# Sixteen heads in a loop over eight pairs, or written out in each engine's program

## What is computed

```python
xn = _layernorm(x, axis=-1)
x = x + attn(xn, Wq, Wkv, Wo, bo) + ffn(xn, gate_W_packed, gate_scales, up_W_packed, up_scales,
                                        down_W_packed, down_scales)
# attn: 16 heads of 32, 4 key/value heads, causal, ALiBi bias, softmax
scores = jnp.einsum('brgtd,bgsd->brgts', qg, k) / jnp.sqrt(jnp.float32(HD))
attn = jax.nn.softmax(jnp.where(causal, scores + bias, -jnp.inf), axis=-1)
out = jnp.einsum('brgts,bgsd->brgtd', attn, v)
# ffn: weights of 4096 x 512 stored as 4-bit codes with a scale for each block of 32
inter = gelu(xt @ Wg.T) * (xt @ Wu.T)
out = inter @ Wd.T
```

## Time and profile before

| | |
|---|---|
| median of three timed runs | 1851.26 us (1844.19 to 1851.6) |
| span of the profiled execution, first to last instruction | 1858.9 us |
| what lies around that span | not given for the profiled execution |
| PE busy | 1758.1 us, 95% of the span |
| DVE busy | 1468.6 us, 79% |
| ACT and POOL busy | 998.6 us and 980.1 us |
| mean granted TensorE clock | 0.980 of full speed |

### The profile page before, as it was taken

How to read it: one execution, slowest core, us unless ns; L and a number is a source line. 1 busy time by engine, 2 the same in 40 slices (tenths; PEclk the granted TensorE clock), 3 DMA queues, 4 the chain that set the end, 5 groups by cost and what they waited for, 6 DMA issues and landing times. The chain is left out here.

```text
span 1858.9 us, 32744 instructions
## 1 busy us (share of the span) xinstructions
PE 1758.1 (95%) x8528; PEld 964.3 (52%) x8528; DVE 1468.6 (79%) x2619; ACT 998.6 (54%) x1722; POOL 980.1 (53%) x785
## 2 busy tenths in 40 slices
PE   4989999999999999999999999999999999999948
PEld 3755555455545555555545554555545554555536
DVE  6878787787868787787868786887868786878848
ACT  2435556464646566464646555564646565564620
POOL 4126556374636556374636465463736464563717
PEclk9999999999999999999999999999999999999979
DMA  6860210202020201202020202102020202002073
GB/s 194 223 153 14 63 25 26 60 20 64 24 61 15 71 17 37 53 16 64 24 66 19 64 15 55 35 16 68 21 66 24 59 16 70 20 20 68 16 196 134
DMA packets 113476, 105.53 MB, mean 57 GB/s; under 512 B 61873, under 2 KB 81329, under 8 KB 111457
## 3 DMA queue, kind: packets, MB, share of 16 engines
q1 hardware_dynamic: 113248, 102.93, 21.2%
HBM read 68.03 MB, written 22.02 MB: 48 GB/s over the span
## 5 line engine op out<-in xcount | busy, mean ns | idle before, releaser
L1269 POOL TENSOR_TENSOR plo<-p,phi 128x512 fp32r<-128x512 f32 (+1 forms) x576 | 710.0, 1237 | 358.7 <-ACT phi L1109 357.0
L1103 ACT ACTIVATE p<-score_ps 128x512 f32<-128x512 f32 (+1 forms) x576 | 328.2, 570 | 382.3 <-DVE score_ps L1188 197.6
L1109 ACT ACTIVATE phi<-p 128x512 fp32r<-128x512 f32 (+1 forms) x576 | 350.2, 608 | 15.2
L1276 POOL TENSOR_TENSOR il<-prod,ih 128x512 f16<-128x512 f32 x128 | 155.4, 1214 | 381.4 <-DVE ih L1175 342.9
L1053 PE MATMUL o_ps<-phi,vst 128*96 128x512 f32 (+3 forms) x640 | 328.1, 529 | 0.0
L1036 PE MATMUL score_ps<-qst,kst 128*128 128x512 f32 (+3 forms) x640 | 318.9, 515 | 0.0
L1202 DVE TENSOR_REDUCE mxp<-max_ps 128x1 f32<-128x512 f32 (+2 forms) x320 | 202.1, 632 | 81.8 <-PE max_ps L1011 43.0
L1181 DVE TENSOR_TENSOR acc<-down_ps,acc 128x512 f32<-128x512 f32 x256 | 174.7, 683 | 74.0 <-PE down_ps L985 72.1
L1053 PE MATMUL o_ps<-plo,vst 128*96 128x512 f32 (+3 forms) x640 | 221.3, 362 | 0.0
L1202 DVE TENSOR_REDUCE mxp<-turn_ps 128x1 f32<-128x512 f32 (+3 forms) x320 | 184.8, 578 | 30.4 <-PE turn_ps L1014 18.5
L998 PE MATMUL gate_ps<-xh,wh 128*128 128x512 f16 x512 | 203.8, 398 | 0.7
(11 more groups left out here) (158 smaller groups left out, 2828.4 us busy)
## 6 DMA issues: line engine op xcount, KB each, us to landing
qst<-q_parts SPq DMA_DIRECT2D x204, 64.0 KB
kst<-k_parts SPq DMA_DIRECT2D x48, 256.0 KB, 4.4
o<-oraw SPq DMA_DIRECT2D x192, 64.0 KB, 2.0
vst<-v_parts SPq DMA_DIRECT2D x17, 512.0 KB, 6.0
q_parts<-o SPq DMA_DIRECT2D x24, 256.0 KB, 3.4
raw<-L_ffn_gate_W_packed_dram SPq DMA_DIRECT2D x18, 256.0 KB, 2.8
raw<-n_L_ffn_up_W_packed_dram SPq DMA_DIRECT2D x18, 256.0 KB, 3.6
raw<-L_ffn_down_W_packed_dram SPq DMA_DIRECT2D x18, 256.0 KB, 4.2
```

Source lines behind the costliest of these rows:

```text
L1103: nc.scalar.activation(p32[n % PR][:, 0:cols], score_ps[:, 0:cols], ACT.Exp).then_inc(exp_done, 1)
L1109: nc.scalar.activation(phi[n % PP][:, 0:cols], p32[n % PR][:, 0:cols], ACT.Copy).then_inc(phi_done, 1)
L1269: nc.gpsimd.tensor_tensor(plo[n % PP][:, 0:cols], p32[n % PR][:, 0:cols], phi[n % PP][:, 0:cols].bitcast(F32), ALU.subtract).then_inc(plo_ ...
L1276: nc.gpsimd.tensor_tensor(il[w % 2][:, a, :], prod[a][:], ih[w % 2][:, a, :], ALU.subtract).then_inc(il_done, 1)
```

## The change

The loop is no longer a hardware loop. `loop` calls `body` sixteen times while the program is built, with `i`, `par` and `pair` as plain numbers. Each engine's program therefore holds the instructions of all sixteen steps one after the other; every wait of the stage is against a constant, every address is a constant, and the register instructions and the branch of L879 are gone. The step's order of work, its tiles, its DMAs and its semaphores are what they were.

The test in `decode_step` is adapted: `before` is now always a number, which is 0 in the preamble and 1 to 16 in the main stage, so the wait on `wf_done` is made in the same cases as before.

```diff
--- before.py
+++ after.py
@@ -259,7 +259,7 @@
 
         if step == 0:
             dve.wait_ge(raw_in[m], (before + 1) * 16)
-            if m or not isinstance(before, int):
+            if m or before:
                 dve.wait_ge(wf_done, before * 6 + 2 * m)
             nc.vector.tensor_scalar(dec[:, 0], raw[m][:], 28, 19, ALU.logical_shift_left,
                                     ALU.arith_shift_right).then_inc(dec_step, 1)
@@ -876,9 +876,8 @@
         reciprocals, add_parts, normalise = output_steps(nc, e)
 
         def loop(eng, body):
-            with eng.Fori(0, HEADS // 2) as pair:
-                for par in range(2):
-                    body(pair * 2 + par, par, pair)
+            for i in range(HEADS):
+                body(i, i % 2, i // 2)
 
 
 
```

## The result

| | before | written out |
|---|---|---|
| median of four timed runs | 1851.43 us (1844.19 to 1855.3) | 1824.83 us (1822.23 to 1826.79) |
| ratio | | 0.9861, 95% interval 0.9836 to 0.9886 |
| span of the profiled execution | 1858.9 us | 1824.5 us |
| mean granted clock in it | 0.980 | 0.987 |

The changed kernel is 26.6 us faster where 35.5 were forecast. It lies at the upper side of the range, 1808 to 1827. From profiled execution to profiled execution the gain in span is 34.4 us, close to the sum; the difference between the two gains is the interesting part of this case.

What follows compares the result with a forecast made beforehand. PE, busy 1758.1 of 1858.9 us, was taken to bound the kernel. 21.0 us of gaps plus 14.5 us of slow clock made 35.5 us, taken from the 1851.3 us median: 1815.8 us, range 1808 to 1827 us.

Steps and rivals of the forecast that it cites:

- The gap: PE's standstill at the seven back edges, where branching engines stand some three microseconds: 21.0 us gained from start to start.
- The clock: Slow matmuls from a step's first to its first down matmul behind seven back edges: 14.5 us gained without gaps.
- From the profiled execution to the median: The 7.6 us between span and median held unrelated to the loop, so the same 35.5 us taken from the median.
- rival A: Seven back edges: gain comes as summed, 1810 to 1820 us, a microsecond or two more either side for registers; chance 0.82.
- rival B: Back edges: part of the gain kept by load-tied slow clock or a shorter stall without profiling; around 1828 us, chance 0.08.
- B's other form: Start of a pair: slow clock tied to the burst of loads, so only 21.0 us go, 1830 us.
- The register instructions: On PE, ACT and DVE inside steps: zero in the sum, ends from about a microsecond's loss to 14.2 us gain.
- Rival E: PE's waits of turn_max for ACT's exponential: registers cost more, most of 14.2 us goes, 1802 us; chance 0.03.
- ACT's table load: Once per loop turn on ACT, 1.28 us, eight times: hidden under gate matmuls, so its going is worth nothing.
- code fetching: Instruction fetches inside steps: a straight program reads as much per step, less register instructions, and the fetching is hidden.
- rival C: Between pieces of an engine's code: straight code fetched late, 5.1 us per late fetch on PE, 1897 us; chance 0.04.
- What is late next: Former back edges: seven transitions take the form of the eight without PE waits, so nothing comes next.

Runs made afterwards that it cites:

- e1: Kernel before with its loop making four turns of four heads (three back edges), waits still in registers: 1839.22 us, ratio 0.9943.
- e2: Kernel before with its loop making two turns of eight heads (one back edge), waits still against registers: 1828.74 us, ratio 0.9887.
- e3: Kernel before with only TensorE's program written out, the four other engines keeping loops of eight turns: 1844.95 us, ratio 0.9977.
- e7: Straight program with TensorE waiting at steps 2, 4, ... 14 until SP's last gather of the step before has landed: 1859.92 us, ratio 1.0051.
- e9: Kernel before, unchanged, profiled once more: 1854.0 us with a span of 1852.0 us.
- e10: Kernel before, unchanged, profiled again for a third sample of seven back edges: 1846.43 us with a span of 1844.6 us.
- e6: Straight program with TensorE waiting at steps 2, 4, ... 14 for DVE's last addition of the step before: 1833.24 us, ratio 0.9903.
- e8: Straight program without POOL's clearing of acc; step 0 copies the down products instead of adding: 1821.07 us, ratio to before 0.9842.

## Why the prediction was right, and where it was off

**The gap.** Right in size and in cause. Forecast 21.0 us over seven edges from start to start; the two further traces of before give 21.7 and 20.3 us by the same measure, and the straight program has none of it. e1 and e2 tie it to the number of edges, and e3 shows what the prediction's reading of PE's branch alone left out: with that branch gone, DVE's still holds TensorE for 15.2 us. One sentence was too wide, that every engine stands for some three microseconds after it has branched back: SP, with the shortest body, does not, 0.23 to 0.27 us.

**The clock.** The mechanism was right: it followed from the standstill, as e7 shows without any branch, and it is absent in the straight program from head 1 to the end of the stage. The size was off, and this is the term that missed. The prediction took 14.5 us from seven windows and said that the losses have two sizes, 1.4 to 1.6 and 2.8 to 2.9 us, so at least 9.8 us in any execution. There is a third size, nothing. e9 and e10 have it behind four of seven edges, and their losses sum to 4.4 and 4.2 us. With their own gaps the sums are 21.7 + 4.4 = 26.1 us and 20.3 + 4.2 = 24.5 us, and the timed runs gained 26.6 and 23.8.

**From the profiled execution to the median.** The prediction saw that the span lay 7.6 us above the median and held that nothing tied this to the loop. It was tied to the loop: an execution's time is 1.7 to 1.9 us more than its span in nearly all runs that list both, so the profiled one had taken some 1861 us (an estimate), at a clock of 0.980, as low as in any execution of before that was listed. That is 9.4 us above the median of 1851.3, and its seven windows hold 10 us more slow clock than those of e9 and e10: about its whole excess was the very term being summed. A hint stood in the table ahead of the prediction: the span alone of this execution was longer than each of the three timed ones.

**The range, and luck.** The forecast as summed, rival A with its spread, ended at 1822 us, and 1824.83 lies outside it. It lies inside 1808 to 1827 only because the upper side was widened for rival B, above all for a stall that would be shorter without profiling. That did not come: e9 and e10, which have the full gaps, are themselves timed executions of 1854.0 and 1846.43 us, as long as the other timed ones. B's other form, slow clock from the burst of loads, is ruled out as well, since the clock is 1.00 in the changed kernel's main stage with the loads where they were. So the width was right for a reason that was wrong, and that part was luck.

**The register instructions.** Priced at nothing, with ends from a loss of about a microsecond to a gain of 14.2 us. They are worth nothing that these runs can tell: the thirty waits for the exponential sum to 15.7 us after 14.2 before, and steps are as long with registers as without, within 0.1 us. Rival E is out.

**ACT's table load, addresses, code fetching.** ACT's seven loads went and its wait for gate matmuls is 165.1 us where it was 164.0: hidden, as said. No gap put down to "issue" stands anywhere in PE's main stage, in a program that fetches 1.71 MB of instructions in all, so rival C is out for this length. That a straight program reads as much per step was wrong: it reads 1.50 MB where the loop read 2.36, a third less, and part of what is gone stood at the back edges, eight packets at the first of them where the straight program has one.

**What is late next.** Nothing, as forecast, but the reason deserves more weight than it got. The prediction argued from PE's branch; e3 shows that DVE's branch was a second stall of nearly the same size under the same gap. Those two programs at least had to be straightened, and the transition inside a pair had shown exactly that case, no engine branching.

**Branches and fetching.** The Trainium skill, Runtime: NRT & Kernel Launch, Instruction fetch mechanics, says that a taken branch out of the window on chip stalls for a fetch. Three traces of before agree: taken branches last up to 4.90 us on PE, eight instruction packets stand at the first back edge of each, and SP, whose body is the shortest, stands for 0.23 to 0.27 us there but for some 3 us once its body is twice as long (e1). The 108 ns that the Trainium skill gives in Advanced Engine Details and Errata, Control Flow Timing, are of the size of a branch that falls through, 0.083 us on PE, and not of PE's taken one, 4.50 us.

What stays open is why the clock falls behind one standstill of some three microseconds and not behind the next. The traces show it behind 7, 3 and 3 of seven edges, with gaps of 2.3 to 3.0 us, and this was not taken further.

## What to carry to other kernels

In a kernel that one engine bounds, compare the same transition with and without a branch: its gap, and the clock behind it, price a loop's back edge, and each engine whose work is needed early in the next turn pays an edge of its own, so straightening one alone moves the wait. The length of an engine's loop body matters too: the one body short enough, SP's, branched back at almost no cost. A clock loss read in one profiled execution is a draw from several; set the span and mean clock of that execution against the timed ones before subtracting it. And once a step's number is a constant, its first turn can differ: here that gave a further 5.6 us.

## What the runs showed that I had not expected

- A standstill of 3.4 us of TensorE was followed by slow clock at five of seven places and one of 0.9 us at none (e7, e6).
- The gap did not follow the length of the body: 3.0 us in the mean at the three edges of e1 against 2.6 us, and 1.8 us at the one edge of e2, behind which PE then waited 1.1 us for DVE, with the clock at 1.00.
- SP stood for 0.3 us at most behind its taken branch with 186 instructions a turn, and for some 3 us with 368 (the trace of before, e1).
- POOL's clearing of `acc`, 6.9 us, held a DVE cast that takes 0.43 us for 6.35 us (e8 against the changed kernel).
